# The rows of every expert tile, turned by transposing transfers into three buffers

## The reference, cut to what matters

```python
x = hidden_states.reshape(-1, dim)                      # 2048 x 256 (h2 in the kernel)
shared_out = _gated_mlp(x, sh_gate, sh_up, sh_down)     # one shared expert for all tokens
top_w, top_idx = jax.lax.top_k(probs, 2)                # two of eight experts for each token
...
for e in range(8):
    h = silu(x @ ex_gate[e].T) * (x @ ex_up[e].T)       # 256 -> 512
    out = out + h @ ex_down[e].T * comb[:, e:e + 1]     # 512 -> 256
return out + shared_out
```

## Time and profile before

| | |
|---|---|
| three runs | 394.14, 395.10, 396.32 us (median 395.1) |
| the profiled execution | 395.73 us |
| its span in the trace | 393.9 us |
| mean granted TensorE clock | 0.991 of 2.4 GHz |
| PE busy | 377.8 us (96%) |
| DVE, ACT, POOL busy | 279.8, 240.5, 199.0 us |

### The profile page before, as it was taken

The page is one execution under the profiler, slowest core; times in us unless marked ns, Lnnn a source line. Parts: engine busy times, 40 slices in busy tenths (PEclk is TensorE's granted clock), DMA queues, the critical chain, the costliest instruction groups (busy, mean ns, idle before and its releaser), DMA issues.

```text
span 393.9 us, 13275 instructions
## 1 busy us (share of the span) xinstructions
PE 377.8 (96%) x5186; PEld 327.4 (83%) x5186; DVE 279.8 (71%) x558; ACT 240.5 (61%) x502; POOL 199.0 (51%) x193
## 2 busy tenths in 40 slices
PE   6989998999999888899999999999999999999997
PEld 3645555778877668899999999999999999999996
DVE  5996487898888785479976676767667675455453
ACT  5588666577667644748477657666666745445432
POOL 2000005777768665311264487768677686663430
PEclk9899999999999999999999999999999999999999
DMA  7954040000292006996421334334334334333233
GB/s 262 351 62 49 2 159 4 2 4 28 75 332 92 29 29 221 328 315 237 84 69 60 78 57 69 57 70 68 56 71 69 69 57 68 69 61 52 29 39 111
DMA packets 26404, 38.81 MB, mean 99 GB/s; under 512 B 5012, under 2 KB 20356, under 8 KB 26216
## 3 DMA queue, kind: packets, MB, share of 16 engines
q1 hardware_dynamic: 16264, 25.53, 21.1%
q0 software_dynamic: 7488, 10.27, 15.7%
q10 hardware_dynamic: 2592, 2.18, 1.6%
HBM read 27.60 MB, written 10.36 MB: 96 GB/s over the span
## 4 chain that ended last, share of the span: by engine, by line
PE 72%; DVE 14%; ACT 6%; issue 4%; ACTq 1%; DMA 1%; DVEq 0%
PE ps L1520 36%; PE ps L1538 18%; PE ps L1328 5%; DVE wx L948 3%; PE ps L1471 3%; DVE tmp L1025 2%; DVE xres L1011 2%; PE ps L1401 1%; DVE st L1014 1%; PE ps L1314 1%; PE ps L1348 1%; DMA tmp<-in_decay_tables 1%; ACT wx L721 1%; DVE st L864 1%; DVE wx L1036 1%
## 5 line engine op out<-in xcount | busy, mean ns | idle before, releaser
L1520 PE MATMUL ps<-tmp,wx 128*128 128x128 bf16 x2640 | 157.0, 219 | 1.4 <-ACT tmp L778 1.4
L1520 PEld LDWEIGHTS ps<-tmp,wx 128*128 (+1 forms) x2640 | 150.1, 98 | 1.6 <-issue 1.5
L542 POOL DMA_INDIRECT out<-tmp,dk x39 | 61.8, 1584 | 46.8 <-DMA out<-tmp,dk 39.5
L787 ACT ACTIVATE tmp<-tmp 128x512 bf16<-128x512 f32 x55 | 34.7, 630 | 80.9 <-PE ps L1538 67.5
L1538 PE MATMUL ps<-wx,tmp 128*128 (+1 forms) x660 | 80.9, 273 | 0.2 <-DVE tmp L1181 0.2
L1175 DVE TENSOR_TENSOR tmp<-ps,tmp 128x512 f32<-128x512 f32 x55 | 38.0, 691 | 57.1 <-PE ps L1520 51.0
L1538 PEld LDWEIGHTS ps<-wx,tmp 128*128 128x128 bf16 x660 | 62.1, 98 | 6.9 <-DVE tmp L1181 0.5
L535 POOL DMA_INDIRECT tmp<-h2rows,src_i x39 | 52.7, 1352 | 12.6 <-issue 10.7
L1181 DVE TENSOR_TENSOR tmp<-tmp 128x512 bf16<-128x512 f32 x55 | 37.8, 688 | 12.5 <-ACT tmp L787 12.4
L948 DVE TENSOR_TENSOR wx<-ps,wx 128x2048 f32<-128x2048 f32 x16 | 36.4, 2275 | 1.9 <-PE ps L1348 1.9
L778 ACT ACTIVATE tmp<-ps 128x512 f32<-128x512 f32 x55 | 32.8, 597 | 5.9 <-PE ps L1520 1.9
(11 more groups left out here) (186 smaller groups left out, 572.8 us busy)
## 6 DMA issues: line engine op xcount, KB each, us to landing
wx<-in_wexp SPq DMA_DIRECT2D x26, 512.0 KB, 5.4
xres<-in_x SPq DMA_DIRECT2D x4, 512.0 KB, 7.9
h2rows<-h2s ACTq DMA_DIRECT2D x16, 128.0 KB, 3.9
out<-h2s SPq DMA_DIRECT2D x12, 128.0 KB
h2s<-in_wmod SPq DMA_DIRECT2D x1, 1024.0 KB, 9.4
wx<-decay_rows SPq DMA_DIRECT2D x16, 64.0 KB
modr<-mod_rows SPq DMA_DIRECT2D x1, 1024.0 KB, 5.0
wx<-in_wqkvu SPq DMA_DIRECT2D x1, 768.0 KB, 8.1
```

Source lines behind the costliest of these rows:

```text
L542: e.indirect_dma_start(t["out"], bass.IndirectOffsetOnAxis(ap=dst_i[:, j:j + 1], axis=0), yb[(NA + j) % 2], None, compute_op=ALU.add).then ...
L787: e.activation(hs[p][:, 0:FF], hf[p], ACT.Copy).then_inc(s["inner_high"], 1)
L1520: ins = e.matmul(half(bank, m * P), weight(at_, weights(part, w) + k * FF + m * P, P), xT[p][:, (2 * a + k) * P:(2 * a + k + 1) * P], star ...
```

## The change

The rows of a tile are no longer turned by PE and copied by ACT. SP starts a transposing transfer from SBUF to SBUF for each of the 55 tiles (`DMA_TRANSPOSE`, 128x512 of 2 bytes), from `h2s` or `xg` straight into one of three buffers `xT`, each with a semaphore of its own (`s_turned`). The transfers stand in SP's list between the loads and stores that were there. The third buffer lies at the end of the tensor that held the projection weights. On POOL, gathers from j = 6 on wait for the result of tile j - 6 (which lies behind the use of the `xg` buffer), and the scatter behind such a gather no longer has a wait of its own for that result.

```diff
-        xT = [at_tmp(i * D, D, bf16) for i in range(2)]
+        xT = [at_tmp(0, D, bf16), at_tmp(D, D, bf16), w_parts[:, KD * 4 * D - D:].bitcast(bf16)]
...
+            def turn_rows(f):
+                if routed(f):
+                    j = f - NA
+                    e.wait_ge(s_xg[j % NXG], 16 * (j // NXG + 1))
+                    rows = xg[j % NXG][:, 0:D].bitcast(bf16)
+                else:
+                    g = shared_of(f)
+                    e.wait_ge(s["h2_high"], g + 1)
+                    e.wait_ge(s["h2_low"], g + 1)
+                    rows = h2s[:, tile_of(g)[0]]
+                wait(e, "up_product", f - NXT + 1)
+                e.dma_start_transpose(xT[f % NXT].rearrange("p (m n) -> p m n", n=P), rows).then_inc(s_turned[f % NXT], 16)
...
             for x in range(3, NE):
                 load_expert(x - 1, x)
+                if x > 3:
+                    turn_rows(x - 1)
             e.wait_ge(s["shared_low"], len(SHARED_PARTS))
             load_expert(NE - 1, 0)
+            turn_rows(NE - 1)
+            turn_rows(NE)
...
+            turned_behind = {NA - 6: (0,), NA - 5: (1,), NA - 4: (2, 3), NA - 3: (4,), NA - 1: (5,)}
             for g in range(NA):
...
+                for j in turned_behind.get(g, ()):
+                    turn_rows(NA + j)
+            for f in range(NA + 6, NF):
+                turn_rows(f)
...
             def gather(j):
-                wait(e, "weight_made", j - NXG + 1)
+                if j < NXG + 2:
+                    wait(e, "weight_made", j - NXG + 1)
+                    if j >= NXG:
+                        f = NA + j - NXG
+                        e.wait_ge(s_turned[f % NXT], 16 * (f // NXT + 1))
+                else:
+                    e.wait_ge(s["result_made"], j - NXG - 1)
...
             def add_rows(j):
                 wait(e, "rows_added", 16 * j)
-                wait(e, "result_made", j + 1)
+                if j + NXG + 2 >= NG:
+                    e.wait_ge(s["result_made"], j + 1)
...
-            def take_rows(f):
-                if is_tile(f):
-                    wait(e, "rows_turned", f + 1)
-                    wait(e, "up_product", f - 1)
-                    e.activation(xT[f % 2], half(ROW_BANK, 0, D).bitcast(bf16), ACT.Copy).then_inc(s["rows_taken"], 1)
...
-                wait(e, "rows_taken", f)
-                for m in range(4):
-                    ins = e.transpose(half(ROW_BANK, 0, D).bitcast(bf16)[:, m * P:(m + 1) * P], rows[:, m * P:(m + 1) * P], identb[:])
-                ins.then_inc(s["rows_turned"], 1)
...
             def gate_or_up(f, part):
-                wait(e, "rows_taken", f + 1)
+                e.wait_ge(s_turned[f % NXT], 16 * (f // NXT + 1))
```

More of the change, by code:

```diff
@@ L38 @@
 NXG = 4
+NXT = 3
 PARTS_AT, SCALED_AT = (2, 9, 11, 13), (0, 1, 2, 3)
@@ L228, in build @@
         order_f = route(NE + 1)
-        assert rused[0] <= KD * 4 * D
+        assert rused[0] <= KD * 4 * D - D
         order = sb("order", [1, NE + 1], i32)
@@ L252, in build @@
                  "shared_loaded down_loaded shared_high shared_low routing routing_exp ranks rows_found "
-                 "low_marked tile_marked marks_weighted rows_turned rows_taken gate_product "
+                 "low_marked tile_marked marks_weighted gate_product "
                  "up_product gate_silu inner_made inner_high inner_low "
@@ L258, in build @@
         s_xg = [sem(f"s_xg{i}") for i in range(NXG)]
+        s_turned = [sem(f"s_turned{i}") for i in range(NXT)]
         s_x = [sem(f"s_xin{g}") for g in range(NT // GT)]
@@ L263, in build @@
         KT_BANK, OUT_BANK, O_BANK, H_BANK = 5, 4, 6, 7
-        ROW_BANK, GATE_BANKS, UP_BANKS, DOWN_BANKS, FREE_BANK = 0, (1, 3), (2, 5), (6, 4), 7
+        GATE_BANKS, UP_BANKS, DOWN_BANKS, FREE_BANK = (1, 3), (2, 5), (6, 4), 7
         block = ctx.enter_context(nc.Block())
@@ L429, in _ @@
             load_expert(1, 2)
+            for f in range(NXT):
+                turn_rows(f)
             e.wait_ge(s["kv_product"], NSTATE)
@@ L450, in _ @@
             e.dma_start(t["out"][B * S:B * S + P, :], xres[:, 0, :]).then_inc(s["x1_stored"], 16)
+            turn_rows(NE + 1)
+            turn_rows(NE + 2)
             e.wait_ge(s["routing"], RT_WEIGHTS)
             e.dma_start(t["h2rows"][:, D:].rearrange("(t p) d -> p t d", p=P), w12.bitcast(u32)).then_inc(s["weights_stored"], 16)
+            turn_rows(NE + 3)
+            turned_behind = {NA - 6: (0,), NA - 5: (1,), NA - 4: (2, 3), NA - 3: (4,), NA - 1: (5,)}
             for g in range(NA):
@@ L821, in _ @@
                     f = n - NT - 1
-                    take_rows(f + 1)
                     middle(f - 1)
@@ L1520, in gate_or_up @@
                         ins = e.matmul(half(bank, m * P), weight(at_, weights(part, w) + k * FF + m * P, P),
-                                       xT[p][:, (2 * a + k) * P:(2 * a + k + 1) * P],
+                                       xT[f % NXT][:, (2 * a + k) * P:(2 * a + k + 1) * P],
                                        start=n == 0, stop=n == 3 * KD - 1)
@@ L1543, in step @@
             def step(f):
-                if is_tile(f + 1) and f + 1 != NA:
-                    turn_rows(f + 1)
                 if is_tile(f):
                     gate_or_up(f, 0)
-                    if f + 1 == NA:
-                        turn_rows(f + 1)
                     gate_or_up(f, 1)
@@ L1599, in _ @@
                     e.wait_ge(s["state_made"], NSTATE)
-                    turn_rows(0)
                     turn_h2(n - 4)
```

## The result

The changed kernel takes 403.81 us (median of 4 runs, 403.18 to 406.15); the kernel before, run beside it, 395.71 (4 runs, 394.14 to 396.32). The ratio is 1.0226, 95% interval 1.0197 to 1.0255: 2.3% slower. The profiled execution took 403.18 us with a span of 401.4, where the working of the prediction came to a span of 392.2.

What follows compares the result with a forecast made beforehand. PE was taken as the bound at 4.21 us a tile, the scatter chain close behind at 4.15. First scatter 223.7, 38 steps to 381.4, end 10.8: span 392.2, 1.7 less than before, so 395.1 - 1.7 = 393.4 us; range 387 to 409.

Steps and rivals of the forecast that it cites:

- The forecast: Whole kernel: scatter steps of 4.10 to 4.25 us, 391.5 to 397 us in all, point 393.4; chance 0.34.
- the rival that the scatter pays for its neighbour: Routed tiles: transfer packets fall among the scatter's, 38 steps by 0.2 to 0.41 us, 401 to 409 us; chance 0.28.
- PE's tile 3.99 in place of 4.21: Routed tiles: without its four transposes of 0.22 us, a tile costs PE 3.99 us instead of 4.21.
- the chain of scatters takes over at once: Routed tiles: the scatter chain, 4.15 us a step, is hidden at PE's 4.21 and would be the bound at 3.99.
- The shared tiles: Before the first routed result: -2.6 transposes, +2.7 stall, +0.2 stall, sum +0.3 us, so first result at 221.
- The stall of 2.7 us at tile 7: Shared tiles: PE waits for tile 7's transfer, queued behind the last expert load; 2.7 us, between 0 and 4.
- The moved wait, "paid once": First scatter: the gather now goes in front, 0.99 + 0.33 us, start at 223.7; delay paid once, later hidden.
- I take 0 for the forecast, because the transfer may be through before the scatter's packets begin: Routed tiles: added cost of the transposing transfers to the scatters, set to 0, the rest left to the range.
- The 4.15: Routed tiles: forecast time from scatter to scatter, in us, ruling over PE's 3.99; last scatter at 381.4.
- My 11 steps of the earlier trace: Later routed tiles before the change: 4 steps of 4.05 and 7 of mean 4.21 us, together 45.66, 4.15 each.
- the 1.3 of the earlier trace: Upper bound for one transfer, from the slowest small-packet transfers: 1.3 us of all engines for 0.13 MB.
- 440: Rival that the transposing transfer is slow in itself: 38 x 1.3 = 49 us, so 440 us; chance 0.13.

Runs made afterwards that it cites:

- e4: Changed kernel with the scatters of even and odd tiles as two chains that don't wait for each other, odd results to another tensor: 391.46 us, ratio 0.9864.
- e8: Kernel before with the scatters of even and odd tiles as two independent chains, odd results to another tensor: 396.14 us, ratio 0.9995.
- e9: Kernel before with only the wait for the result moved from the scatter to the gather, PE still turning the rows: 399.94 us, ratio 1.0105.
- e3: Changed kernel with the wait for the result put back from the gather to the scatter: 403.19 us, ratio 1.0181.
- e10: Changed kernel without the transposing transfers of the 39 routed tiles and with the wait for the result back on the scatter: 396.54 us, ratio 1.0021.
- e6: Changed kernel with each routed transfer held until POOL has issued the next gather, the last four until a scatter has landed: 397.86 us, ratio 1.0037.
- e5: Kernel before without PE's transposes and ACT's copies for the 39 routed tiles, products formed from rows left in buffers: 392.72 us, ratio 0.9904.
- e1: Changed kernel without the transposing transfers of the 39 routed tiles, products formed from rows left in buffers: 399.77 us (395.69 to 403.04), no ratio.
- e11: Repeat of e1, the changed kernel without the transposing transfers of the 39 routed tiles: 396.89 us, ratio 1.0044.
- e2: Changed kernel with a plain SBUF to SBUF copy of the same 128 KB in place of each transposing transfer: 400.13 us, ratio 1.0111.

## Why the prediction was wrong

The forecast (the same or a little faster, 393.4) fell, and the rival that the scatter pays for its neighbour came true, within its 401 to 409. That the number fell into this range is partly luck: the rival let all 38 scatters pay 0.2 to 0.4 us, and 7 paid 0.9. Step by step:

- **PE's tile 3.99 in place of 4.21: right**, and that the chain of scatters takes over at once: right, shown by e4 and e8.
- **The shared tiles: sum right, place not.** First result 220.53, forecast 221. The stall of 2.7 us at tile 7 was 1.53, with two smaller ones in front (0.78 and 0.83, the transfers of two tiles that I had let pass free); together 3.14.
- **The moved wait, "paid once": right for the first scatter, too small for the rest.** The first scatter started 2.22 behind its result; I had 2.68. But e9 shows that the same delay, on a kernel where PE sets the pace, costs 4.3 us: the slack between a landing and the result that needs its buffer had absorbed late landings, and the gather in front of the scatter uses it up. In e9 it is the 9 steps with an instruction packet that grow, from 4.30 to 4.74; why these most, no run tells. In the changed kernel the slack is gone anyhow, which fits that e3 and e10 find the place of the wait worth nothing.
- **"I take 0 for the forecast, because the transfer may be through before the scatter's packets begin": the step that failed.** The scatters' step was 4.39, not 4.15; 38 x 0.24 = 9.1 of the 9.2 us by which the span missed (401.4 against 392.2; the first scatter was 0.95 early, the end 1.1 longer). The transfers don't take a little from every scatter, as the rival had it, either. 28 steps took 4.16. The 7 with a transfer's packets in front of the scatter's took 5.06, which is 7 x 0.91 = 6.4 us over 4.15; in two of them, 6.10 and 5.98, an instruction packet has a share that I can't separate. 3 with an instruction packet alone make 2.4 more. e6 got 6 us back by holding the transfers until their phase was harmless. I had worked out the place, 0.65 to 3.55 behind a scatter's start, across its packets, and then priced it by its mildest reading.
- **The 4.15 itself was right for undisturbed steps and a little low for the mean.** The 28 undisturbed steps took 4.16. Without any routed transfer the mean is 4.18 (e5) and 4.22 to 4.35 (e10, e1, e11), with the instruction packets in it. My 11 steps of the earlier trace rows held one late one (351.83 to 356.72, with such a packet).
- **The price of a transfer.** By the profile's page, q1's share grew from 21.1% of 393.9 us to 31.2% of 401.4, 42.1 us for 55 transfers: 0.77 us of all engines each. In the window from 335.4 to 340.4 it was 20.0% of 5 us, 1.0, while other packets were waiting; in e6, from 334.4 to 338.5, 13.8% of 4.1 us, 0.57. The nearest row that I had, a plain store at 0.41, is that of the plain copy of e2, 0.39, and half of the transposing one; the 1.3 of the earlier trace rows was too high. And 38 x 1.3 added to 393.4 is 443, not 440.

The Trainium skill (DMA: Bandwidth & Descriptors, Latency and other measured facts) gives 261 GB/s, by which I had estimated 0.50 us: the transfer with little beside it, 0.57, nearly agrees. The Trainium skill (DMA: Bandwidth & Descriptors, Issuing engines are not separate DMA queues) also says that transfers from SP and POOL run on the same 16 engines; the rows of the late step agree with it, in which q0 gets 22 packets through beside 487 of q1.

What is shown and what only argued: that the landings are the bound and that the phase of the transfers costs 6 to 7 us is shown by runs (e4, e8; e6, e11). That a late scatter without a transfer in front of it is held up by an instruction packet rests on the order of the packets in the traces, not on a run that changed it; and a few late steps have neither (in e11 one of 4.55). Left open are some 4 us: e10 (396.5) has no routed transfers and the wait of before, and still stands that much behind e5 (392.7), from which it differs in the 16 shared tiles, turned by transfers and not by PE, and in the buffers and waits that go with them. 2.05 us of it are there at the first scatter (222.44 and 220.39), so among the shared tiles; no run has these alone. No kernel with the whole computation beat the one before.

## What to carry to other kernels

Before work is taken off the bounding engine, measure how far behind it the next chain stands, over all its steps and not over its quiet stretch: that distance, here 3.5 us of the 8.6 in e5, is what there is to win while the chain stays. A transfer moved to shared DMA engines is priced by when its packets come, not by its bytes alone; if its place falls in front of packets that a chain waits for, take it as paid, or tie its issue to an event that keeps it out of their way. Slack that looks idle may be absorbing late landings.

## What the runs showed of the hardware

- A transposing transfer of 128x512 values of 2 bytes from SBUF to SBUF goes as 544 packets of some 240 bytes (131 KB), takes 0.57 us of all 16 engines with little beside it and up to 1.0 in company. SP mostly needs 1.19 us to issue one, at most 2.29; by the line's instructions (count: shortest, median, longest in ns):

```profile
L438 SPq DMA_TRANSPOSE tmp<-tmp x26: 1189/1192/2287, 202.4 to 357.6; - x26
```

- Issued 0.4 to 0.8 us behind the start of a scatter by POOL (128 rows of 1 KB), it went in front of the scatter's rows in all six steps of the changed kernel; the first row went 2.34 to 2.60 us behind the start in place of 2.12 to 2.25, and the step was 0.3 to 1.8 us longer than 4.16. Issued at 0.95 to 1.18 it went beside or behind them, and five of six steps were 4.21 to 4.26. Issued at 0.16 and 0.26 it was through before them (4.10 and 4.20).
- One 16 KB packet of the queue named instruction was in flight for up to 1.8 us beside a scatter (292.00 to 297.45), and 8 of the 128 rows went only behind it.
- A gather's 0.99 us on POOL was 1.9 to 2.0 in 11 of 39 tiles (293.89 above). It cost nearly nothing: in nearly all steps the landing that the next scatter waited for came so late that the longer gather didn't matter, and in the others it cost 0.2 us or less.
